# Attention and expert routing of layer 1 in one stage, routed batch by batch, with expert weights in the head buffers

## The chip, the cores and the metric

The kernel runs on one core of a Trainium2 chip. The metric is device time in microseconds (us) for one execution. Engine names are those of the profile: PE is TensorE (PEld its weight loads), DVE is VectorE, ACT is ScalarE, POOL is GpSimd, SP is SyncE, whose queue issues most DMAs.

## The reference

Four sub-layers follow one another on 4 x 1024 tokens of width 128: a Mamba mixer, a dense-routed expert layer, causal attention with 16 heads of 8, and a 64-expert top-4 layer. A layer norm follows each. The change touches the last two:

```python
scores = jnp.where(causal_mask, -1e9, einsum('bhqk,bhsk->bhqs', q, k) / sqrt(dk))
ctx = einsum('bhqs,bhsk->bhqk', softmax(scores), v)
x = layernorm(x + concat(ctx) @ Wo + bo)
top_p, top_i = top_k(softmax(x @ router_w), 4)
# slot of a (token, expert) pair: the count of earlier tokens that chose the expert
buf[expert, slot] = x[token]                     # 64 experts x 128 slots
y = (silu(buf @ w1[..., :64]) * (buf @ w1[..., 64:])) @ w2
x = layernorm(x + sum over the four chosen y * top_p)
```

## The kernel before, in words

The program is a chain of stages, each a block of its own with a barrier behind it. The last five are `attn_project` (941 to 1003 us), `attn_scores` (1003 to 1524), `out_and_route` (1524 to 1748), `moe_experts` (1748 to about 1845) and `moe_combine` (to 1903.7).

**`attn_scores`** handles 16 groups: group gi is 4 heads of batch gi // 4. The work of a group has two passes. The first pass finds row maxima: 39 items (`item`, L1762 and L1765 on PE into one of 3 PSUM banks; `first_pass`, L1688 on DVE reads the bank and frees it). It runs two groups ahead of the second pass. The second pass goes through 12 blocks of keys (`BLOCKS`, index n). For each block PE makes scores of two head pairs (`scores`, L1782), ACT takes their exponentials (L1665), POOL masks the 8 blocks on the diagonal (L1637), and PE multiplies with V three blocks later (`product`, L1797, `LAG` = 3). ACT copies the context of each half (L1654), PE turns it (`turn_context`, L1806), and DVE divides by the sums (`divide`, L1715 and L1719). PE's order is written out by `ring`: each block has four places x = 0 to 3, scores stand at 0 and 1, the product at 2, and the items are spread over all four; every other use of the 3 banks (the turned maxima, the turned contexts) has a fixed place too. PE works in program order, so any wait stops what is behind it. Batches 1 and 2 are two rounds of one hardware loop (`Fori` in `batches`); batches 0 and 3 are written out.

**`out_and_route`** then works on the four batches (quarters) one by one. PE turns the context (L2125), adds the bias with a one-row matmul (L2135) and multiplies by Wo (L2137). DVE adds the residual and norms (L2021 to L2035), PE turns again and makes the router's logits (L2148), and DVE finds the top four, the one-hot masks `oh`, the counts and the slots (`top_four`, `place`, `probabilities`, `share_beyond`), with two matmuls for running counts between (L2154, L2155). POOL scatters the quarter's rows to the DRAM tensor `slots`, one indirect DMA for each of 8 tiles x 4 choices (L1971): 32 a quarter, 128 in all. At the stage's start SP zeroes `slots` and loads w1 and w2, POOL clears w2's buffer (L1963), and small tables are made.

**`moe_experts`** loads `slots` (L2208) only behind the barrier, so it starts after the last scatter.

## Time and profile before

| | us |
|---|---|
| median of 3 runs (lowest, highest) | 1907.59 (1906.0, 1912.56) |
| the profiled execution | 1905.42 |
| its span | 1903.7 |
| attention stage | 1003 to 1524 |
| route stage | 1524 to 1748 |
| PE / DVE / ACT / POOL busy in the span | 1352.0 / 1315.3 / 881.0 / 842.4 |

The span is what the profiler sees between the first and the last instruction; the execution's own time is 1.7 us longer. The busy shares are means over very different stages, so the table of the row section that splits the span by stage says more. PEclk there is the granted TensorE clock: 1.00 is 2.4 GHz, 0.50 is 1.2 GHz.

### The profile page before, as it was taken

The numbers are of one execution on the slowest core, as the hardware profiler recorded it, in microseconds if no ns is written. First come the engines' busy times: TensorE is split into PE (matmuls) and PEld (weight loads), VectorE is DVE, ScalarE is ACT, GpSimd is POOL, SyncE is SP. The second block draws the span as 40 slices with busy tenths as digits, with TensorE's granted clock in tenths as the row PEclk, the third lists the DMA queues.
The fourth block names the chain that finished last, engine by engine and source line by source line (L and its number), as shares of the span: only waits on it lengthen the run. The fifth ranks groups of instructions, "written<-read, shape, count | busy, mean of one in ns | idle before, by whom it ended". The sixth has DMA issues, their size and how long they took to land. (4 is left out here: it accounts for less than half of the span.)

```text
span 1903.7 us, 27622 instructions
## 1 busy us (share of the span) xinstructions
PE 1352.0 (71%) x7253; PEld 734.7 (39%) x7253; DVE 1315.3 (69%) x2625; ACT 881.0 (46%) x1585; POOL 842.4 (44%) x930
## 2 busy tenths in 40 slices
PE   6847677677778669996236999999999944401637
PEld 2313333233333358996122344443444233201634
DVE  7999999999995351335648788887888167710315
ACT  5845565555655425563130566665666711101420
POOL 1666676666762045616430212121121217774750
PEclk8969999999999879998577899999999955555868
DMA  1000000000006226875052011010110091001315
GB/s 49 0 1 0 1 1 0 1 0 1 0 1 269 82 81 193 242 205 151 25 147 80 26 39 54 35 48 35 47 46 11 2 231 43 24 12 41 102 49 207
DMA packets 112117, 122.77 MB, mean 64 GB/s; under 512 B 28263, under 2 KB 87768, under 8 KB 108177
## 3 DMA queue, kind: packets, MB, share of 16 engines
q1 hardware_dynamic: 90480, 99.81, 17.0%
q0 software_dynamic: 10240, 15.79, 2.8%
q10 hardware_dynamic: 11264, 5.60, 1.0%
q8 instruction: 59, 0.97, 0.2%
q14 instruction: 74, 0.60, 0.1%
HBM read 76.62 MB, written 50.52 MB: 67 GB/s over the span
## 5 line engine op out<-in xcount | busy, mean ns | idle before, releaser
L1688 DVE TENSOR_REDUCE t_negm<-t_ps 128x1 f32<-128x512 f32 (+4 forms) x624 | 366.5, 640 | 63.3 <-PE t_ps L1765 39.9
L1665 ACT ACTIVATE t_PT<-t_ps_s 128x1024 f32<-128x1024 f32 (+3 forms) x384 | 293.1, 812 | 208.9 <-PE t_ps_s L1782 208.4
L435 POOL TENSOR_TENSOR s_HC<-s_H,s_C_sb 128x512 f32<-128x512 f32 x256 | 323.0, 1283 | 147.8 <-DVE s_H L523 125.7
L1637 POOL TENSOR_SCALAR_AFFINE_SELECT t_PT<-t_PT 128x512 f32<-128x512 f32 x128 | 80.5, 635 | 399.2 <-ACT t_PT L1665 399.2
L554 PE MATMUL ps_y<-s_HC,ident 128*128 128x512 f32 x512 | 252.0, 616 | 1.3 <-POOL s_HC L435 1.2
L1762 PE MATMUL t_ps<-c_K,c_Q 128*128 128x512 bf16 (+3 forms) x768 | 232.2, 341 | 27.5 <-DVE t_identb L1681 16.6
L473 ACT ACTIVATE s_dA<-m_DT,s_A 128x512 f32 (+1 forms) x256 | 169.9, 711 | 91.4 <-DVE s_H L523 91.1
L1782 PE MATMUL t_ps_s<-c_Q,c_K 128*128 128x512 bf16 (+3 forms) x768 | 181.9, 330 | 10.1 <-DMA c_Q<-max_parts 3.8
L540 PE MATMUL ps_b<-m_G,s_sel 128*128 (+1 forms) x128 | 74.3, 580 | 146.0 <-DVE s_H L523 125.4
L1971 POOL DMA_INDIRECT slots<-X,r_idx_s x128 | 129.4, 1011 | 82.4 <-issue 41.3
L1797 PE MATMUL t_ps_c<-t_PT,t_VG 128*32 128x512 f32 (+3 forms) x1536 | 163.4, 499 | 0.6 <-ACT t_CT L1654 0.6
L1762 PEld LDWEIGHTS t_ps<-c_K,c_Q 128*128 128x128 bf16 x768 | 74.3, 100 | 185.4 <-DVE t_negm L1688 133.9
L992 ACT ACTIVATE f_HT<-f_ps_h,f_b 128x128 f32<-128x128 f32 x340 | 96.5, 370 | 81.7 <-PE f_ps_h L1264 80.5
L554 PEld LDWEIGHTS ps_y<-s_HC,ident 128*128 128x128 f32 x512 | 101.4, 198 | 83.6 <-issue 64.2
L540 PEld LDWEIGHTS ps_b<-m_G,s_sel 128*128 128x128 f32 x128 | 25.6, 200 | 243.0 <-DVE s_H L523 183.1
L962 POOL DMA_INDIRECT f_YG<-expert_rows_out,f_idx_s x64 | 66.2, 1034 | 87.3 <-DMA expert_rows_out<-f_YB 68.7
L1765 PE MATMUL t_ps<-t_mask,t_identb 128*128 128x128 bf16 x512 | 104.4, 229 | 0.0
L1264 PE MATMUL f_ps_h<-f_XT,f_w 128*128 128x128 f32 x680 | 92.2, 280 | 8.1 <-issue 7.2
L1782 PEld LDWEIGHTS t_ps_s<-c_Q,c_K 128*128 128x128 bf16 x768 | 64.3, 98 | 72.8 <-ACT t_PT L1665 24.9
L1279 PE MATMUL f_ps_y<-f_w,f_HT 128*128 x680 | 89.8, 276 | 1.7 <-ACT f_HT L992 1.7
L1120 DVE COPY f_YB<-f_ps_y 128x512 f32<-128x512 f32 (+1 forms) x22 | 14.7, 669 | 109.1 <-PE f_ps_y L1279 100.6
L1264 PEld LDWEIGHTS f_ps_h<-f_XT,f_w 128*128 128x128 f32 x680 | 84.2, 195 | 9.8 <-issue 9.8
(323 smaller groups left out, 2525.2 us busy)
## 6 DMA issues: line engine op xcount, KB each, us to landing
f_w<-in_W_dram SPq DMA_DIRECT2D x93, 256.0 KB, 4.4
c_Q<-qk_parts SPq DMA_DIRECT2D x48, 192.0 KB
c_K<-qk_parts SPq DMA_DIRECT2D x48, 192.0 KB
token_expert_rows<-k_zero SPq DMA_DIRECT2D x8, 1024.0 KB, 10.2
y_Y<-token_expert_rows SPq DMA_DIRECT2D x8, 1024.0 KB, 7.9
qk_parts<-p_parts SPq DMA_DIRECT2D x48, 128.0 KB, 2.4
f_XS<-expert_rows SPq DMA_DIRECT2D x19, 256.0 KB
expert_rows_out<-f_YB ACTq DMA_DIRECT2D x19, 256.0 KB
```

Of the source, the lines that this page charges most:

```text
L435: nc.gpsimd.tensor_tensor(HC[:, g % RING, c, :], H[:, k, c, :], C_sb[:, k, :], ALU.mult).then_inc(s_hc, 1)
L473: nc.scalar.activation(dA[:, k, c, :], chunk2(DT, c, i), ACT.Exp, scale=A[:, c, g:g + 1]).then_inc(s_da, 1)
L540: nc.tensor.matmul(ps_b[k][:], sel[:, g, :], chunk(G, i), start=True, stop=True).then_inc(s_b, 1)
L554: nc.tensor.matmul(ps_y[c][:], ident[:], HC[:, g % RING, c, :], start=g == 0, stop=g == N - 1, skip_group_check=True).then_inc(s_y, 1)
L1264: mm = nc.tensor.matmul(ps_h[k % RH][:, m * P:(m + 1) * P], w1[:, k % RW, m * P:(m + 1) * P], XT[:, q % 2, a * P:(a + 1) * P], start=True, ...
L1665: nc.scalar.activation(PT[:, n % RP, 2 * p:2 * p + 2, 0:w], src, ACT.Exp, scale=DK ** -0.5).then_inc(s_exp, 1)
L1688: nc.vector.tensor_reduce(out, ps_1[bank][:, 0:h * width].rearrange("p (h k) -> p h k", h=h), AX.X, ALU.max, negate=True).then_inc(s_mx, 1)
L1762: mm = nc.tensor.matmul(ps_1[bank][:, u * width:(u + 1) * width], Q[g][:, j + u, qt * P:(qt + 1) * P], K[g][:, j + u, c * CH:c * CH + widt ...
L1765: mm = nc.tensor.matmul(ps_1[bank][:, (u + 1) * width - P:(u + 1) * width], identb[:], mask[:], start=False, stop=True, skip_group_check=True)
L1782: mm = nc.tensor.matmul(ps_s[p][:, h * CH:h * CH + w], K[g][:, 2 * p + h, kt * P:(kt + 1) * P], Q[g][:, 2 * p + h, c * CH + r * P:(c + 1) ...
L1797: mm = nc.tensor.matmul(ps_c[j * VW:(j + 1) * VW, r * P:CH], VG[:, g % 2, kt, j * VW:(j + 1) * VW], PT[:, n % RP, j, 0:w], start=kt == 0, ...
L1971: pool.indirect_dma_start(out=slots, out_offset=bass.IndirectOffsetOnAxis(ap=idx_s[:, j, t:t + 1].bitcast(U32), axis=0), in_=XM[:, t, :], ...
```

## The change

`attn_scores` and `out_and_route` become one stage, `attend_and_route`. The loop over batches 1 and 2 is gone: all 16 groups are written out. While batch q+1 is attended, batch q is routed, by this table: in group 0 of the next batch PE turns the context (before block 6) and multiplies by Wo (blocks 8 and 9), and DVE takes the statistics; in group 1 DVE norms, PE turns (before block 5) and makes the logits (block 7), and DVE chooses; in group 2 PE makes the counts (blocks 0 and 1) and DVE the slots. DVE does one step of a routine behind each use of a bank from the third on, and the rest of the routine at the group's end. The turned rows use the two score buffers `ps_s`; the other matmuls take turns in the 3-bank ring. POOL scatters one tile's choice per block, from group 2, block 6 on; what is left of the third batch follows the last group, then the clearing of w2, then the last batch's 32 scatters. The last batch is routed behind the last group with nothing beside it.

The bias is no longer a matmul: POOL adds `bo` to a batch's residual rows in group 1 of its own batch. ACT's table switches for the square root and back fall between exponentials. `slots` is zeroed in the attention stage behind the first maxima. The experts' w1 and w2 have no buffers of their own: w1 is loaded into the Q and K buffers of head groups 0 and 1 after the last batch's group 1, w2 into those of groups 2 and 3 after the last scores. The context rows and `oh` lie in the buffer `X2`. `moe_experts` and `moe_combine` are as before.

```diff
+ROUTE = [("out", 0, 0, 8, 3), ("out", 1, 0, 9, 3), ("logits", 0, 1, 7, 3), ("rank", 0, 2, 0, 3), ("rank", 1, 2, 1, 3)]
+TURN = [(0, 6), (1, 5)]
+TURNS = [(NG * (q + 1) + g, n) for q in range(BATCH - 1) for g, n in TURN]
+SCATTER = (2, 6)
...
+            if gi + 2 < TG:
+                uses += [("item", i, n, x) for i in range(NI * at // (4 * NB), NI * (at + 1) // (4 * NB))]
+            if at == 3 and gi + 1 < TG:
+                uses.append(("max", 0, n, x))
+            if x == 2 and n == LAG + 1 and gi:
                 uses.append(("context", 1, n, x))
             if x == 2 and n == LAG + 5:
                 uses.append(("context", 0, n, x))
+            if gi >= NG:
+                uses += [(kind, i, n, x) for kind, i, *when in ROUTE if when == [gi % NG, n, x]]
...
-        def batches(eng, body, first=0):
-            if first:
-                body(0, False)
-            with eng.Fori(first, BATCH - 1) as b:
-                body(b, False)
-            body(BATCH - 1, True)
...
+            maxima(0)
+            sp.wait_ge(s_m, 8)
+            for q in range(8):
+                rows = slots[q * (SLOTS // 8):(q + 1) * (SLOTS // 8), :].rearrange("(p a) n -> p (a n)", p=P)
+                sp.dma_start(rows, zero).then_inc(s_zb, 16)
+            for gi in range(TG):
+                b, g = gi // NG, gi % NG
+                if gi + 1 < TG:
+                    maxima(gi + 1)
+                sp.wait_ge(s_st, pair_use(gi, NB - 1) + 2)
+                if b + 1 < BATCH:
+                    sp.wait_ge(s_ml[g], b * 16 + 16)
+                    load_heads(sp, dram, keep, b + 1, g, dram["zeros"])
+                elif g == 1:
+                    for e in range(0, E1, GE):
+                        sp.dma_start(keep["w1"][:, e:e + GE, :], io["w1"][e:e + GE].rearrange("e d f -> d e f")).then_inc(keep["s_ew"], 16)
+            sp.wait_ge(s_zw, 1)
+            for q in range(2):
+                src = io["w2"].rearrange("(c q) i n -> q i c n", q=2)[q]
+                sp.dma_start(w2[q * I1:(q + 1) * I1, q:E1:2, :], src).then_inc(keep["s_ew"], 16)
...
+            def scatter(k):
+                q, t, j = k // (QTR * TOPK), k // TOPK, k % TOPK
+                if k == 0:
+                    pool.wait_ge(s_zb, 16 * 8)
+                if k % (QTR * TOPK) == 0:
+                    pool.wait_ge(s_x, q + 1)
+                    pool.wait_ge(s_nt, 2 * q + 2)
+                pool.indirect_dma_start(out=slots, out_offset=bass.IndirectOffsetOnAxis(ap=idx_s[:, j, t:t + 1].bitcast(U32), axis=0),
+                                        in_=XM[:, t, :], in_offset=None, bounds_check=SLOTS - 1, oob_is_err=False).then_inc(s_sc, 16)
+            sent = 0
+            for gi in range(TG):
+                for n, (c, kt, r) in enumerate(BLOCKS):
+                    if n == 2 and gi + 1 < TG:
+                        v_group(gi + 1)
+                    if n == 5 and gi % NG == 1:
+                        if gi < NG:
+                            pool.wait_ge(s_w, 48)
+                        rows = X[:, gi // NG * QTR:(gi // NG + 1) * QTR, :]
+                        nc.gpsimd.tensor_tensor(rows, rows, row_wide(bo[:], QTR), ALU.add).then_inc(s_bo, 1)
+                    if kt >= c * PER:
+                        pool.wait_ge(s_exp, pair_use(gi, n) + 2 + AHEAD)
                         part = PT[:, n % RP, :, 0:P]
                         nc.gpsimd.affine_select(out=part, in_=part, compare_op=ALU.is_ge, fill=0.0, base=0,
                                                 pattern=[[0, GH], [1, P]], channel_multiplier=-1).then_inc(s_mk, 1)
-            batches(pool, body)
+                    if gi * NB + n >= (NG * (sent // (QTR * TOPK) + 1) + SCATTER[0]) * NB + SCATTER[1]:
+                        scatter(sent)
+                        sent += 1
+            while sent < QTR * TOPK * (BATCH - 1):
+                scatter(sent)
+                sent += 1
+            pool.wait_ge(s_st, pair_use(TG - 1, NB - 1) + 2)
+            nc.gpsimd.memset(w2.rearrange("p e n -> p (e n)"), 0.0).then_inc(s_zw, 1)
+            while sent < QTR * TOPK * BATCH:
+                scatter(sent)
+                sent += 1
+            pool.wait_ge(s_sc, 16 * TOPK * NT)
...
+            def turned(q, k):
+                for p in range(2):
+                    act.wait_ge(s_st, turn_use(q, k) + p + 1)
+                    if k:
+                        act.wait_ge(s_p1, route_use(q, "out", p) + 1)
+                    elif q:
+                        act.wait_ge(s_p1, route_use(q - 1, "logits") + 1)
+                    nc.scalar.activation(CXT[:, p, :], ps_s[p][:, 0:CH], ACT.Copy).then_inc(s_exp, 1)
...
+                    if q >= 0 and (gi % NG, n) in TURN:
+                        turned(q, TURN.index((gi % NG, n)))
+                    if q >= 0 and (gi % NG, n) == (1, 0):
+                        root(q)
+                    if q >= 0 and (gi % NG, n) == (2, 0):
+                        route_exp(q)
...
+            for gi in range(TG):
+                q = gi // NG - 1
+                beside = normalise(q) if q >= 0 and gi % NG == 1 else iter(())
+                for k, (kind, i, *_) in enumerate(USES[gi]):
+                    use = BEGIN[gi] + k
+                    if kind == "item":
+                        first_pass(gi + 2, i, use)
+                    elif kind == "max":
+                        parts(gi + 1, use)
+                    elif kind == "context":
+                        divide(gi - i, i, use)
+                    elif kind == "out":
+                        projected(q, i, use)
+                        if i:
+                            beside = statistics(q)
+                    elif kind == "logits":
+                        logits_copy(q, use)
+                        beside = choose(q)
+                    elif i == 0:
+                        counts(q, use)
+                    else:
+                        positions(q, use)
+                        beside = place(q)
+                    if k >= 2:
+                        next(beside, None)
+                for _ in beside:
+                    pass
+            q = BATCH - 1
+            divide(TG - 1, 1, use_of(TG, "context", 1))
+            for h in range(2):
+                projected(q, h, route_use(q, "out", h))
+            for _ in statistics(q):
+                pass
+            for _ in normalise(q):
+                pass
+            logits_copy(q, route_use(q, "logits"))
+            for _ in choose(q):
+                pass
+            counts(q, route_use(q, "rank", 0))
+            positions(q, route_use(q, "rank", 1))
+            for _ in place(q):
+                pass
...
-def out_and_route(nc, io, keep, slots):
...
+            def turn_rows(q, k):
+                if k:
+                    pe.wait_ge(s_n, (q + 1) * QTR)
+                else:
+                    pe.wait_ge(s_mx, use_of(NG * (q + 1), "context", 1) + 1 + BANKS1)
+                for p in range(2):
+                    pe.wait_ge(s_exp, turn_use(q, k) + p - 1 + AHEAD)
+                    for t in range(PER):
+                        row = XM[:, q * QTR + p * PER + t, 0:P] if k else CX[:, q % 2 * QT + p * PER + t, :]
+                        mm = nc.tensor.transpose(ps_s[p][:, t * P:(t + 1) * P], row, ident[:])
+                    mm.then_inc(s_st, 1)
...
+            def project(q, h, use):
+                pe.wait_ge(s_w, 48)
+                pe.wait_ge(s_exp, turn_use(q, 0) + h + 1 + AHEAD)
+                pe.wait_ge(s_mx, use + 1)
+                for t in range(PER):
+                    mm = nc.tensor.matmul(ps_1[use % BANKS1][:, t * P:(t + 1) * P], CXT[:, h, t * P:(t + 1) * P], w[:], start=True, stop=True)
+                mm.then_inc(s_p1, 1)
...
+        QK = ctx.enter_context(nc.sbuf_tensor("heads", [P, 2 * NG, GH, SEQ], BF16))
+        flat = lambda lo, hi: QK[:, lo:hi].rearrange("p a j t -> p (a j t)").bitcast(F32)
+        half = 2 * QT * P
+        own = dict(keep, QK=QK, s_ew=ctx.enter_context(nc.semaphore("expert_weights")),
+                   w1=flat(0, NG).rearrange("p (e n) -> p e n", n=2 * I1), w2=flat(NG, 2 * NG).rearrange("p (e n) -> p e n", n=P),
+                   CX=keep["X2"][:, 0:half].rearrange("p (t n) -> p t n", n=P),
+                   oh=keep["X2"][:, half:T].rearrange("p (j t e) -> p j t e", j=TOPK, e=E1))
+        attention(nc, io, own, slots)
```

Three places show how instructions moved. The first is DVE in group 1 of a batch that has a batch to route (the third batch here), from the turned context of the first half on; `t_negm<-t_ps` is a first-pass item, `t_LG` the logits, `X` under L1916 the one-hot masks. Before, items follow one another:

```order
L1715 RECIPROCAL t_den<-t_ps 128x16
L1719 TENSOR_TENSOR CX<-t_ps,t_den 128x32 x4
L1688 TENSOR_REDUCE t_negm<-t_ps 128x4
L1688 TENSOR_REDUCE t_negm<-t_ps 128x2 x2
L1688 TENSOR_REDUCE t_negm<-t_ps 128x1 x8
L1693 TENSOR_TENSOR t_negm<-t_negm 128x4x4
```

Now:

```order
L1831 TENSOR_TENSOR X<-t_ps,t_den 128x32 x4
L1907 CAST t_idxf<-t_idx 128x64
L1908 TENSOR_TENSOR over<-t_LG,t_top 128x512
L1909 TENSOR_TENSOR t_ex<-t_top 128x32
L1911 COPY X<-t_idxf 128x8x4
L1798 TENSOR_REDUCE t_negm<-t_ps 128x4
L1916 TENSOR_TENSOR X<-t_iota,t_idxf 128x512 x2
L1798 TENSOR_REDUCE t_negm<-t_ps 128x2
L1916 TENSOR_TENSOR X<-t_iota,t_idxf 128x512 x2
L1798 TENSOR_REDUCE t_negm<-t_ps 128x2
L1921 TENSOR_TENSOR t_pair<-X 128x512 x2
```

One or two route steps now stand between each two items that PE waits to see read.

The second place is DVE in group 14, where no first-pass items are left. Before, the maxima of group 15 (L1700 to L1708) and then the divisions alone:

```order
L1702 CAST t_mp<-t_msb 32x128
L1704 TENSOR_TENSOR t_mrest<-t_msb,t_mp 32x128
L1706 CAST t_mp<-t_mrest 32x128
L1708 TENSOR_TENSOR t_mp<-t_mrest,t_mp 32x128
L1715 RECIPROCAL t_den<-t_ps 128x16
L1719 TENSOR_TENSOR CX<-t_ps,t_den 128x32 x4
```

Now, from the positions on:

```order
L1941 TENSOR_TENSOR t_pos<-t_ps,t_base 128x512
L1948 TENSOR_TENSOR X<-X,t_pos 128x512 x2
L1826 RECIPROCAL t_den<-t_ps 128x16
L1831 TENSOR_TENSOR X<-t_ps,t_den 128x32 x4
L1948 TENSOR_TENSOR X<-X,t_pos 128x512 x2
L1826 RECIPROCAL t_den<-t_ps 128x16
L1831 TENSOR_TENSOR X<-t_ps,t_den 128x32 x4
L1952 TENSOR_REDUCE t_posj<-X 128x32
```

The slots of the third batch (L1952 and what follows) come behind both divisions, the second of which waits for PE's block 8.

The third place is POOL at the end. Before, groups 14 and 15 had the masks and a copy alone, and the next stage began with its tables:

```order
L1637 AFFINE_SELECT t_PT<-t_PT 128x4x128 x8
L1620 COPY t_VG<-c_Vt 128x4x8 x8
L1637 AFFINE_SELECT t_PT<-t_PT 128x4x128 x14
L1528 UNCONDITIONAL_BRANCH
L1953 UNCONDITIONAL_BRANCH
L1955 MEMSET r_ones_row 1x128
```

Now, from the last diagonal blocks of group 15 on:

```order
L1713 AFFINE_SELECT t_PT<-t_PT 128x4x128
L1697 DMA slots<-X,t_idx_s 8192x140
L1713 AFFINE_SELECT t_PT<-t_PT 128x4x128
L1697 DMA slots<-X,t_idx_s 8192x140 x15
L1722 MEMSET heads 128x8192
L1697 DMA slots<-X,t_idx_s 8192x140 x32
```

A scatter stands behind each mask, and 14 scatters and the clearing of w2 stand ahead of the last batch's 32.

## Rows read from the trace of the kernel before

**Rows 1.** The table by stage; the columns are named in its first line.
```profile
core 0: us, PE busy (x) PEld busy (x) DVE busy (x) ACT busy (x) POOL busy (x), PEclk, DMA share, GB/s
...
1172.20:1290.90 118.70, 117.56 (x932) 49.62 (x932) 102.21 (x221) 76.53 (x105) 24.93 (x64) 1.00 0.12 44
...
1524.00:1574.00 50.00, 26.11 (x82) 17.48 (x82) 31.72 (x94) 8.39 (x12) 9.44 (x7) 0.54 0.87 220
1574.00:1676.00 102.00, 36.17 (x135) 26.33 (x134) 80.47 (x271) 15.26 (x24) 78.02 (x76) 0.52 0.10 32
```

**Rows 2.** Waits in four steady groups: total us, times, longest (DVE, weight loads).
```profile
DVE t_negm L1688 <- PE t_ps L1765: 8.0, 20, 0.6
...
PEld t_ps L1762 <- DVE t_negm L1688: 30.3, 49, 0.8
```

**Rows 3.** Timeline of SyncE: the first head load behind groups 7 and 8.
```profile
1290.97 0.77 SPq L1353 DMA_DIRECT2D c_Q<-qk_parts  x1
...
1325.83 0.80 SPq L1353 DMA_DIRECT2D c_Q<-qk_parts  x1
```

**Rows 4.** Timeline of the route stage's first quarter, setup and chain.
```profile
1527.14 6.92 POOL L1963 MEMSET experts_w<- 128x8192 f32 x1
1527.22 7.12 DVE L2000 CAST r_iota<-r_iota_i 128x512 f32<-128x512 int32 x1 [2.97 <-POOL r_trif L1961]
...
1534.86 1.94 PE L2125 MATMUL r_ps_t<-ident,CX 128*128 128x128 f32 x8 [11.42 <-DVE X L2004]
...
1536.73 2.07 PE L2135 MATMUL r_ps_o<-r_bo,r_ones_row 1*128 1x512 f32 x2
...
1537.45 1.28 ACT L1989 ACT_TABLE_LOAD   x1
...
1538.73 2.08 PE L2137 MATMUL r_ps_o<-r_w,r_CXT 128*128 128x128 f32 x8
...
1541.65 0.87 DVE L2024 BATCH_NORM_STATS2 r_stats<-X2t 128x6 f32<-128x128 f32 x4
...
1546.37 0.63 DVE L2027 BATCH_NORM_AGGREGATE r_mv<-r_stats 128x2 f32<-128x6 f32 x8
...
1547.71 2.13 DVE L2035 TENSOR_SCALAR X<-X2t,r_mv,r_rstd 128x128 f32<-128x128 f32 x8
...
1550.81 3.55 PE L2148 MATMUL r_ps_l<-r_router,r_CXT 128*128 128x64 f32 x16
...
1554.39 0.69 DVE L2041 COPY r_LG<-r_ps_l 128x512 f32<-128x512 f32 x1 [4.55 <-PE r_ps_l L2148]
...
1562.57 0.69 DVE L2086 TENSOR_TENSOR r_M<-r_pair 128x512 bf16<-128x512 f32 x1
...
1564.39 2.01 DVE L2090 TENSOR_TENSOR r_base<-r_base,r_ps_n 128x64 f32<-128x64 f32 x8 [1.13 <-PE r_ps_p L2155]
...
1575.12 1.30 POOL L1971 DMA_INDIRECT slots<-X,r_idx_s  x1 [41.06 <-DVE X L2061]
```

**Rows 5.** One tile, slots: the scatter, and the first load of the experts.
```profile
L1971 POOL DMA_INDIRECT slots<-X,r_idx_s x128: 981/982/1502, 1575.1 to 1744.8; - x128
L2208 SPq DMA_DIRECT2D e_x<-slots x16: 359/360/501, 1748.7 to 1804.7; - x16
```

**Rows 6.** Timelines of groups 14 and 15: POOL's masks, DVE, ACT.
```profile
1493.37 0.64 POOL L1637 TENSOR_SCALAR_AFFINE_SELECT t_PT<-t_PT 128x512 f32<-128x512 f32 x1 [10.49 <-ACT t_PT L1665]
...
1493.89 0.48 DVE L1719 TENSOR_TENSOR CX<-t_ps,t_den 128x32 f32<-128x32 f32 x4
...
1523.77 0.48 DVE L1719 TENSOR_TENSOR CX<-t_ps,t_den 128x32 f32<-128x32 f32 x4
...
1497.14 0.66 ACT L1665 ACTIVATE t_PT<-t_ps_s 128x256 f32<-128x256 f32 x2 [0.48 <-PE t_ps_s L1782]
...
1522.14 0.60 ACT L1673 ACTIVATE t_CT<-t_ps_c 128x512 f32<-128x512 f32 x1 [1.77 <-PE t_ps_c L1797]
```

**Rows 7.** One tile, r_zero: how long zeroing the slots takes to land.
```profile
DMA to landing us min/median/max: 2.8/5.2/6.9
```

770 lines of the change are left out of this document (330 added, 440 removed).

## Prediction

> **What bounds the kernel now.** I read the table by stage first, since the shares over the whole span mix unlike stages. The reader is to see two things in it. In attention TensorE is busy 117.56 of 118.70 us in four groups at a clock of 1.00, and VectorE 102.21 of them; a group takes 118.7 / 4 = 29.7 us, of which VectorE works 25.5 [rows 1]. In the route stage nothing is full: VectorE works 31.72 of 50 us and then 80.47 of 102, after which POOL alone is left with its scatters [rows 1]. The timeline of that stage shows its chain [rows 4]: tables, projection, norm, logits, choice, slots, and the first scatter at 1575.12. The rows of the tile slots give the rest: 128 scatters start from 1575.1 to 1744.8, so one in 169.7 / 127 = 1.34 us, and the experts' first load starts at 1748.7 [rows 5]. Attention ends with VectorE's last division at 1523.77 + 0.48 = 1524.3 [rows 6], so the route stage is 224.4 us of one engine waiting for another, half-clocked on TensorE (0.54 and 0.52) [rows 1].
>
> Attention must be read with the waits. TensorE is busy by the page, yet its weight loads waited 30.3 us in four groups for VectorE's reads of a bank, and VectorE 8.0 us (the largest of its waits) for the items [rows 2]. So the two are coupled through three banks: what is added to either shows in part.
>
> **What goes.** After the change only the last batch is routed outside attention. Its tail is a chain and 32 scatters.
> - The chain from the first turned context to the first scatter took 1575.12 - 1534.86 = 40.3 us [rows 4]. The tables ahead of it, 10.6 us of which 7.12 are one cast, are made in attention now, at its start, where VectorE is waited for by nothing late. The bias matmuls, 2.07 us for each half [rows 4], are gone, 4.1 in all; but VectorE now takes the first half's statistics (0.87) behind both additions and no longer beside the second half's product, so 3.2 off. TensorE comes out of attention at 1.00, so that the first turns (1.94) and one multiplication by Wo (2.08) [rows 4] may take half: 1.5 off, an estimate. Against that, clearing w2 now falls into the chain. Before, VectorE's cast started at 1527.22 beside POOL's clearing that started at 1527.14 and ran 6.92 us, and it took 7.12 [rows 4]: it ended 0.28 us after it. By POOL's order in the new program 14 scatters x 1.34 = 19 us come first, so the clearing meets the logits' copy and the top-four work. Bounds 0 and 6.9; I take 2, since most operations there are not of that cast's kind. Chain: 40.3 - 3.2 - 1.5 + 2 = 37.6.
> - Scatters: 31 x 1.34 = 41.4, and from the last one's start to the experts' load 1748.7 - 1744.8 = 3.9 [rows 5].
> - Tail 82.9 us against 224.4: **141.5 gained**.
> - Batches 1 and 2 were rounds of a hardware loop. The head loads behind groups 7 and 8 start 1325.83 - 1290.97 = 34.9 us apart [rows 3], where a group takes 29.7: the jump costs 5.2 us. Written out it goes: **5.2 gained**. The groups inside the loop take 29.7, as those of batch 0 do, so nothing else changes with it.
>
> **What is added to attention.** VectorE's route work for a batch is 31.72 + 80.47 us less 7.12 for the cast and 0.8 for small tables, over four: 26.1 busy [rows 1, 4]. With the gaps of its own chain it splits by the table of the change:
> - Group 0: two additions at 0.69, eight statistics (0.87 for four), 0.63 for their means and 0.17: 3.9 [rows 4].
> - Group 1: norm 2.4 (2.13 and a reciprocal), and from the logits' copy at 1554.39 to the end of M at 1563.26: 8.9. Together 11.3 [rows 4].
> - Group 2: from 1564.39 to the scatter at 1575.12, 10.7, and of the three last operations, 0.69 each, the part behind it, 1.3: 12.0 [rows 4].
>
> TensorE's part at half clock is 1.94 + 2 x 2.08 in group 0 and 2.14 + 3.55 in group 1 (2.14 is the second set of turns, taken as the first set plus 0.2) [rows 4]. At full clock that is 3.1 and 2.8, with a copy by ScalarE between each turn and the next scores, 0.6 (the context copy's time) [rows 6].
>
> A group has 29.7 us and VectorE needs 25.5 of it. With route work it needs 29.4, 36.8 and 37.5. Lower bound of a group's growth: 0 for the first, 7.1 and 7.8 for the others (VectorE never idle). Upper bound: all of it in a row, 3.9 + 3.7, 11.3 + 3.4 and 12.0 + 0.6. I stand near the lower: in the steps that are too long for the banks TensorE fills all three, which feed VectorE for 3 x 0.69 = 2.1 us, more than a product or a pair of scores takes between items. I take +4 (TensorE's own 3.7 lies there), +8.5 and +9: 21.5 for a batch, **43** for two.
>
> In the third, groups 0 and 1 cost the same 12.5. Group 2 is group 14, with no items to spread the work over. The slots of that batch come behind the second division, which ended at 1494.37 [rows 6]; then comes what is left of group 2's 10.7 us to the scatter once the counts (2.0), the positions (0.7) and four multiplications (4 x 0.69) are out [rows 4]: 5.3, to 1499.7. POOL stands at block 6 for it, and masks of blocks 8 to 11 are queued behind two scatters: the first mask would end at 1499.7 + 2 x 1.34 + 0.64 = 1503.0, where it ended at 1494.0 [rows 6]. PE's product wants it when block 11 is scored, about when ScalarE starts that block at 1497.1 [rows 6]: 5 to 6 us of stall, with the scores of group 15 behind it. From there a mask and a scatter take 2.0 us, as long as a wide block but more than a narrow one, which adds 2 to 3 by the last mask: **8** (bounds 4 and 13). Sum of the third: 20.5.
>
> ScalarE loads its tables twice more in a batch, 1.28 each [rows 4]; it works 76.53 of 118.70 us [rows 1], and in groups 1 and 2, where VectorE is the later one, that is covered. If VectorE were not late, it would cost up to 2.6 a batch. POOL's addition of the bias, on 128x1024 elements where a mask has half as many (0.64 [rows 6]), takes at least 1.3 us; four times that, 5 us, is my upper bound, and it stands among blocks 4 to 7, which need no mask: covered. In full batches a mask and a scatter (2.0 us) fit a block of 2.5: covered, by the three blocks that a product lags. Zeroing the slots lands within 6.9 us of its issue [rows 7] and the maxima of group 1 have some 20 us: covered; w1 and w2 land well before the tail's end. Three small loads ahead of the head loads: +1, an estimate.
>
> **Sum.** Attention +43 + 20.5 + 1 - 5.2 = +59.3; tail -141.5; together -82. The profiled execution took 1905.4, so 1823; the median of before stands 2.2 above it, so **1825**.
>
> **A row and a page against this change.** The row that speaks against overlapping VectorE with POOL is the cast of 7.12 us, which ended 0.28 us after a clearing of 6.92 us on POOL [rows 4]. It bears on the tail, where the sum has 2 us for it, and with the whole clearing it would have 6.9 and end at 1830. The Trainium skill, "SBUF — State Buffer", section "Who interferes with whom", says that the two engines share a pair of ports, held by one instruction for its whole length, by copies and casts of VectorE above all. By that page the operations of the top-four part that are copies or casts would wait for the clearing. The cast agrees with it; no row shows the other kinds beside POOL.
>
> **Rivals.**
> 1. *The gaps take it up.* VectorE idles 118.70 - 102.21 = 16.5 us in four groups [rows 1]. If all is used and TensorE's part is hidden, a batch grows by 26.1 - 16.5 = 9.6 to 11: attention 3 x 10 + 8 + 1 - 5 = +34, time 1800. Against it: groups 0 and 3 can't lend their gaps to 1 and 2. Chance 0.13.
> 2. *Nothing is covered.* Work of VectorE, TensorE and the table loads in a row: 27 + 7 + 2.6 = 37 a batch, 111 + 8 + 1 - 5 = +115, time 1881. For it: the coupling in [rows 2]. Against it: VectorE does not wait long anywhere. Chance 0.15.
> 3. *Masks and route steps collide.* A batch has fifteen 128x512 operations of VectorE that read two SBUF tiles, and if each waits for a mask (0.64 [rows 6]), that is 10 us a batch, 30 in all, time 1855. Masks fill 25 of 119 us on POOL [rows 1], so one in five would meet. Chance 0.07. The same section of the Trainium skill states this collision as a rule; no row here shows it.
> 4. *Scatters hold up TensorE: slower.* POOL's masks queue behind scatters. If a mask comes later than the three blocks that a product waits, each of the 96 scatters in attention moves TensorE by its whole 1.34 us: 129 on top of rival 2's 115: +244 - 141 = 2010. It decides from the point where a mask and a scatter together (2.0 us) exceed a block's time (2.5 us). Chance 0.03.
>
> **Chances.** The forecast has 0.62. Only rival 4 is slower. A measurement of this kernel tells 0.3% from no change. Faster 0.965, same 0.005, slower 0.03. The range takes in rival 1 and 3, 1798 to 1858, and leaves out rivals 2 and 4 with 0.18.
>
> **What would show it.** Right: groups of 33 to 34, 38, 38.5 and 29.7 us in batches 1 and 2, with VectorE over 95% busy in the second and third; no jump of 5 us between batches 1 and 2; POOL's first mask of group 14's last four some 8 us behind ScalarE; a tail of 83 us from the last division to the experts' load. Wrong: groups 1 and 2 of 30 to 35 us (rival 1), of over 43 (rival 2), or TensorE waiting for POOL in every batch (rivals 3 and 4).

## The result and the profile after

| | before | after |
|---|---|---|
| median of 4 runs, us | 1909.49 | 1853.22 |
| lowest, highest | 1906.0, 1912.56 | 1852.22, 1857.57 |
| span of the profiled execution | 1903.7 | 1851.0 |
| last division to the experts' first load | 224.4 | 85.9 |

The ratio is 0.9714, 95% interval 0.9700 to 0.9728: 56 us faster, where 82 were forecast. The time after lies inside the range, 28 us above the predicted 1825. The runs e1_unroll to e8_all below were timed while every kernel, before included, took some 130 us longer (before 2049 us), and e9_w2_late to e12_after_again while before took 1910, so runs are compared within these two sets, and by stage.

In the traces the last division of attention ends at 1609.64 where it ended at 1524.25: attention and what lies ahead of it are 85.4 us longer (59.3 forecast). The tail is 138.5 us shorter (141.5 forecast). The table by stage of the changed kernel comes first, cut where SP issues the next head loads, so one row is one group, 4 to 11, then groups 12 and 13, groups 14 and 15, and the tail. A group took 29.7 us before [rows 1]. The columns are the time and its length, then busy us (instructions) of PE, PEld, DVE, ACT and POOL, the granted clock, the DMA share and GB/s.

```profile
core 0: us, PE busy (x) PEld busy (x) DVE busy (x) ACT busy (x) POOL busy (x), PEclk, DMA share, GB/s
1176.54:1209.43 32.89, 32.38 (x257) 15.06 (x255) 27.74 (x65) 20.41 (x29) 6.26 (x16) 1.00 0.11 40
1209.43:1254.29 44.86, 37.54 (x258) 16.18 (x259) 38.77 (x113) 23.55 (x32) 8.84 (x17) 0.87 0.08 29
1254.29:1295.79 41.50, 34.42 (x236) 12.69 (x235) 36.07 (x81) 19.82 (x28) 12.69 (x21) 0.89 0.10 38
1295.79:1325.46 29.67, 29.34 (x234) 12.36 (x233) 25.43 (x57) 19.31 (x27) 18.07 (x29) 1.00 0.21 72
1325.46:1358.41 32.95, 32.39 (x257) 15.08 (x255) 27.80 (x65) 20.41 (x29) 17.98 (x29) 1.00 0.18 61
1358.41:1402.15 43.74, 36.80 (x258) 16.16 (x259) 38.70 (x114) 23.55 (x32) 13.49 (x21) 0.90 0.09 35
1402.15:1444.72 42.57, 34.69 (x236) 12.77 (x235) 36.19 (x81) 19.93 (x28) 12.66 (x21) 0.91 0.09 34
1444.72:1474.40 29.68, 29.34 (x234) 12.36 (x233) 25.45 (x57) 19.33 (x27) 18.07 (x29) 1.00 0.17 59
1474.40:1550.85 76.45, 68.56 (x515) 30.48 (x514) 66.07 (x176) 43.93 (x60) 30.30 (x49) 0.96 0.07 23
1550.85:1609.64 58.79, 47.96 (x349) 13.84 (x347) 19.69 (x61) 39.14 (x56) 31.82 (x44) 0.94 0.31 79
1609.64:1695.50 85.86, 9.80 (x50) 7.95 (x50) 29.48 (x91) 5.80 (x9) 51.09 (x46) 0.55 0.18 30
```

The growth sits in group 1 of a batch (44.9 and 43.7 us) and group 2 (41.5 and 42.6). VectorE has 38.7 us of work in the first and 36.1 in the second, so neither engine is full: VectorE stands idle for 5.0 to 6.4 us of each. TensorE, busy 29.3 us in a plain group, now shows 34 to 38 at a mean clock of 0.87 to 0.91; group 2 has almost the same matmuls, group 1 has 24 more for the routing. (With the clock at 1.00, in e10_even_last below, groups 5 and 6 show 32.6 and 31.0.) The waits of groups 5 and 6 together (us in all, times, the longest) show who waits:

```profile
PEld t_ps L2043 <- DVE t_negm L1798: 26.2, 28, 2.8
PE t_ps L2043 <- DVE t_negm L1798: 10.7, 10, 2.5
...
DVE t_negm L1798 <- PE t_ps L2046: 6.1, 8, 1.5
...
DVE t_negm L1798 <- PE t_ps L2043: 3.4, 6, 0.6
```

How one such wait goes is seen in group 5 at 1215. VectorE's order of time (start, us), then four slices of 4 us:

```profile
1215.48 1.11 DVE L1883 TENSOR_SCALAR X<-X2t,t_mv,t_rstd 128x128 f32<-128x128 f32 x4
1216.51 0.27 DVE L1809 COPY t_msb<-t_ps 32x128 f32<-32x128 f32 x1
...
1218.17 1.10 DVE L1883 TENSOR_SCALAR X<-X2t,t_mv,t_rstd 128x128 f32<-128x128 f32 x4
1219.20 2.06 DVE L1798 TENSOR_REDUCE t_negm<-t_ps 128x2 f32<-128x512 f32 x4
```

```profile
1214.00:1218.00 4.00, 3.20 (x31) 1.65 (x29) 3.51 (x12) 2.78 (x4) 1.27 (x2) 1.00 0.19 80
1218.00:1222.00 4.00, 2.07 (x15) 0.99 (x16) 3.82 (x10) 0.69 (x2) 0.00 (x0) 0.62 0.22 85
1222.00:1226.00 4.00, 4.00 (x19) 1.29 (x20) 2.08 (x3) 1.37 (x3) 3.78 (x11) 0.53 0.19 80
1226.00:1230.00 4.00, 4.00 (x30) 2.23 (x28) 3.20 (x9) 2.10 (x3) 1.03 (x1) 1.00 0.07 24
```

And TensorE in order of time, its wait, then a product of eight wide matmuls; the last line is such a product in a group of batch 0:

```profile
1219.93 0.50 PE L2043 MATMUL t_ps<-heads 128*128 128x384 bf16 x1 [2.48 <-DVE t_negm L1798]
...
1224.05 1.89 PE L2077 MATMUL t_ps_c<-t_PT,t_VG 128*32 128x512 f32 x8
...
1142.39 1.07 PE L2077 MATMUL t_ps_c<-t_PT,t_VG 128*32 128x512 f32 x8
```

Two norm steps with the maxima's chain between them fill 3.7 us, in which VectorE reads one bank only (the copy at 1216.51). TensorE fills its three banks and stands for 2.48 us. In slices of 1 us its granted clock is 0.97 at 1218, 0.50 from 1219 to 1225, and 1.00 again from 1226: it falls to 1.2 GHz while TensorE still stands, and stays there for some 6 us. In the last 4 of these TensorE is the later engine: the eight products take 1.89 us, not 1.07, and VectorE is busy for 2.08 us of 4. So this lump of route work costs twice, once as TensorE's wait and once as VectorE's wait for a half-clocked TensorE. The top four at 1245 to 1258 show the same. At the slots, 1265 to 1280, TensorE waits and the clock falls to 0.50 too, but VectorE is busy for 9.7 of the 10 us from 1270 on, so there the low clock costs nothing.

The low clock is not all of it. Of the 6.1 us that VectorE idles in group 5, 2.4 lie at half clock. Another 2.9 lie between 1228 and 1240 at a clock of 1.00: the norm is done, the logits are not there yet, TensorE is busy almost throughout, and VectorE's gaps hold no route work. So the work is too dense in one place and absent in another.

### The profile page after: what moved, and what is told of

Same layout as the page of the kernel before. It is cut to its first block and busy times, and to the rows that moved or that the text cites. A ratio compares the mean times of both kernels' runs of the same rounds, so it can differ in the third digit from the quotient of the medians.

```text
span 1851.0 us, 25866 instructions
## 1 busy us (share of the span) xinstructions
PE 1347.2 (73%) x7237; PEld 721.1 (39%) x7237; DVE 1312.3 (71%) x2628; ACT 883.2 (48%) x1585; POOL 853.5 (46%) x933
## 5 line engine op out<-in xcount | busy, mean ns | idle before, releaser
L1798 DVE TENSOR_REDUCE t_negm<-t_ps 128x1 f32<-128x512 f32 (+4 forms) x624 | 371.2, 641 | 68.0 <-PE t_ps L2046 38.6
L2043 PE MATMUL t_ps<-heads 128*128 128x512 bf16 (+3 forms) x768 | 239.3, 349 | 59.1 <-DVE t_negm L1798 39.0
L2062 PE MATMUL t_ps_s<-heads 128*128 128x512 bf16 (+3 forms) x768 | 185.7, 336 | 8.0 <-DMA heads<-max_parts 4.2
L2077 PE MATMUL t_ps_c<-t_PT,t_VG 128*32 128x512 f32 (+3 forms) x1536 | 172.2, 523 | 6.9 <-POOL t_PT L1713 6.3
L2043 PEld LDWEIGHTS t_ps<-heads 128*128 128x128 bf16 x768 | 74.7, 101 | 229.7 <-DVE t_negm L1798 164.2
L1697 POOL DMA_INDIRECT slots<-X,t_idx_s x128 | 126.9, 992 | 76.1 <-DVE X L1964 43.4
L992 ACT ACTIVATE f_HT<-f_ps_h,f_b 128x128 f32<-128x128 f32 x340 | 96.7, 371 | 82.9 <-PE f_ps_h L1264 81.6
L2062 PEld LDWEIGHTS t_ps_s<-heads 128*128 128x128 bf16 x768 | 66.0, 101 | 73.7 <-ACT t_PT L1774 22.3
L1120 DVE COPY f_YB<-f_ps_y 128x512 f32<-128x512 f32 (+1 forms) x22 | 14.7, 670 | 111.2 <-PE f_ps_y L1279 97.2
```

The lines of the kernel that those rows point to most:

```text
L1697: pool.indirect_dma_start(out=slots, out_offset=bass.IndirectOffsetOnAxis(ap=idx_s[:, j, t:t + 1].bitcast(U32), axis=0), in_=XM[:, t, :], ...
L1798: nc.vector.tensor_reduce(out, ps_1[use % BANKS1][:, 0:h * width].rearrange("p (h k) -> p h k", h=h), AX.X, ALU.max, negate=True).then_inc ...
L2043: mm = nc.tensor.matmul(out[:, u * width:(u + 1) * width], Q[g][:, j + u, qt * P:(qt + 1) * P], K[g][:, j + u, c * CH:c * CH + width], sta ...
L2062: mm = nc.tensor.matmul(ps_s[p][:, h * CH:h * CH + wd], K[g][:, 2 * p + h, kt * P:(kt + 1) * P], Q[g][:, 2 * p + h, c * CH + r * P:(c + 1) ...
L2077: mm = nc.tensor.matmul(ps_c[j * VW:(j + 1) * VW, r * P:CH], VG[:, g % 2, kt, j * VW:(j + 1) * VW], PT[:, n % RP, j, 0:wd], start=kt == 0, ...
```

## The experiments

In the first set most of the 130 us lies ahead of attention: the first head load is issued at 1194 us in e2_group14 and at 1088 in the changed kernel. The first groups of attention, which have no route work, kept their 29.6 us. But groups 7 and 11 took 30.7 and group 8 36.8 in e2_group14, where the changed kernel has 29.7 and 33.0; e9_w2_late of the second set, with the same edit, has 29.7 and 33.0 again. So that excess isn't from an edit, and its cause stays open.

**The loop written out, alone** (kernel before).

```diff
-            if first:
-                body(0, False)
-            with eng.Fori(first, BATCH - 1) as b:
-                body(b, False)
-            body(BATCH - 1, True)
+            for b in range(BATCH):
+                body(b, b == BATCH - 1)
```

> The kernel before with its attention loop over batches 1 and 2 written out, nothing else. By the prediction's term the back edge goes: 5.2 us less (ratio 0.9973), head loads behind groups 7 and 8 29.7 us apart and no longer 34.9, all other groups 29.6 to 29.7. Rival: the longer program loses as much in loading its code; then 0 in all, and single groups or the stage's start are longer.

Ratio 0.9988 (0.9963 to 1.0013), too coarse for 5 us. The trace tells it: SP's head loads behind groups 7 and 8 start at 1405.73 and 1435.35, 29.6 us apart, where they were 34.9 [rows 3], and all other groups take 29.6. So the jump of 5.2 us is gone from the trace, and no group is longer. Whether the stage's start pays something for it can't be told, since before has no trace in this set.

**Slots of batch 2 at once.**

```diff
                         positions(q, use)
                         beside = place(q)
+                        if gi + 2 == TG:
+                            for _ in beside:
+                                pass
```

> The changed kernel, with the slots of batch 2 made at once behind the positions in group 14 (that group has no items between which the steps could lie), not step by step behind later uses. If TensorE's 5.7 us wait for a mask in group 14 is from the slots being late, the first scatter of that batch starts 5 to 8 us earlier, the wait falls under 2 us, and the kernel is 5 to 8 us faster than the changed kernel's 1853 (1845 to 1848). Rival: the mask and scatter pace of 2.0 us sets the length of groups 14 and 15 in any case; then the wait moves on to later blocks and the kernel stays within 2 us of 1853.

Groups 14 and 15 take 52.0 us and no longer 58.8. POOL's scatter, which stood 16.32 us for the slots in the changed kernel, stands 7.08. First the changed kernel, then this one (start, us, and in brackets the idle time before it):

```profile
1576.87 1.38 POOL L1697 DMA_INDIRECT slots<-X,t_idx_s  x1 [16.32 <-DVE X L1964]
...
1579.52 0.65 POOL L1713 TENSOR_SCALAR_AFFINE_SELECT t_PT<-t_PT 128x512 f32<-128x512 f32 x1
...
1580.23 1.93 PE L2077 MATMUL t_ps_c<-t_PT,t_VG 128*32 128x512 f32 x8 [5.73 <-POOL t_PT L1713]
```

```profile
1680.82 1.38 POOL L1697 DMA_INDIRECT slots<-X,t_idx_s  x1 [7.08 <-DVE X L1964]
...
1663.59:1715.60 52.01, 46.63 (x349) 13.58 (x347) 19.50 (x60) 39.08 (x56) 31.67 (x44) 0.99 0.33 89
```

The scatter pace was not the bound there. TensorE's longest wait for a mask in these groups is 0.65 us, where it was 5.73. The rival falls, and 6.8 us are won. This kernel is the base of what follows.

**Steps further apart.** The base here is the changed kernel; a step runs behind every second use in group 1 and every fourth in group 2.

```diff
+EVERY = {1: 2, 2: 4}
...
-                    if k >= 2:
+                    if k >= 2 and k % EVERY.get(gi % NG, 1) == 0:
                         next(beside, None)
```

> The changed kernel, with a route step behind every second use of a bank in group 1 and every fourth in group 2, not behind every one: the same work, spread over the group. Lumps: route steps that come one after another starve TensorE, which then runs at half clock, so spreading them takes groups 6 and 10 from 41.5 and 42.6 us to 37 or 38 (VectorE's busy time there is 36), and 8 to 11 us off the kernel (1842 to 1845). Rival, additive: VectorE and TensorE pass three banks to and fro, so each us of route work shows wherever it stands; then groups 5, 6, 9, 10 keep their lengths within 1 us and the kernel stays at 1853. In both cases group 14, which has few uses, gets its slots later, 3 to 8 us worse.

Groups 5 and 6 of e2_group14, then of this kernel:

```profile
1315.72:1359.43 43.71, 36.47 (x258) 15.88 (x259) 38.73 (x113) 23.54 (x32) 8.82 (x17) 0.90 0.08 29
1359.43:1402.15 42.72, 34.71 (x236) 12.69 (x235) 36.13 (x81) 19.92 (x28) 12.67 (x21) 0.90 0.10 37
```

```profile
1317.54:1354.47 36.93, 33.04 (x257) 14.87 (x257) 33.17 (x105) 23.29 (x32) 8.55 (x17) 1.00 0.09 35
1354.47:1396.72 42.25, 33.36 (x236) 13.00 (x237) 40.94 (x89) 20.34 (x28) 10.84 (x21) 0.96 0.10 38
```

The first theory forecast 37 or 38 us for groups 6 and 10; they took 42.3 both, so it had the place wrong. The additive rival had groups 5 and 9 unchanged, and it fails too. The pair went from 86.4 to 79.2 us with the same work: the end of the top-four part (the last compares, the sums and M) slipped from group 5 into VectorE's time of group 6 (33.2 and 40.9 us busy in place of 38.7 and 36.1), VectorE's idle time fell from 11.6 us to 5.1, and the clock in group 5 is 1.00. Groups 9 and 10 took 39.6 and 42.3. This is group 9:

```profile
1463.01:1502.63 39.62, 35.72 (x257) 15.52 (x257) 33.47 (x105) 23.42 (x32) 12.14 (x21) 0.91 0.11 38
```

It has nearly the busy time of group 5 on VectorE (33.5 and 33.2 us), and in both TensorE stands for 1.4 us at the norm, before 1327.0 and before 1472.5. But in group 5 the clock stays at 1.00, and in group 9 it is 0.50 from 1474 to 1479, and the group is 2.7 us longer. That is the price of one fall of the clock by itself, as far as one pair of groups can show it. At it the two falls that begin in group 5 of the changed kernel come to some 5 us, an estimate. What e3_spread won in these groups it lost in groups 14 and 15, 65.6 us, as expected; the median is the same as that of e2_group14 (1977.3 and 1976.9).

**More VectorE work.**

```diff
                     also(nc.vector.tensor_tensor(oh[:, j], iota[:], wide(idxf[:, :, j], E1), ALU.is_equal))
+                    link(nc.vector.tensor_tensor(M[:], iota[:], wide(idxf[:, :, j], E1), ALU.is_equal))
...
+                    link(nc.vector.tensor_tensor(pair[:, 1], iota[:], pos[:], ALU.mult))
                     also(nc.vector.tensor_tensor(oh[:, j], oh[:, j], pos[:], ALU.mult))
```

> The changed kernel, with four more compares of 0.68 us (into a buffer that is overwritten) in the choice of a batch (group 1) and four more products of 0.69 us in its slots (group 2): 2.7 us more in each. Additive: groups 5, 9 and 13 grow by 2.7 each, groups 6, 10 and 14 by 2.7, the tail by 5.5: +22 us, 1875. Clock: each added us of VectorE also keeps TensorE waiting and lowers its granted clock, so groups grow by 4 or more each and the kernel by 30 or more. Gaps: VectorE was idle for 5 to 6 us of such a group, so under half of it shows in attention: +14 or less.

```profile
1321.64:1368.67 47.03, 36.79 (x258) 16.00 (x259) 41.75 (x117) 23.54 (x32) 8.81 (x17) 0.87 0.07 27
1368.67:1415.41 46.74, 37.02 (x236) 13.52 (x235) 39.99 (x85) 19.92 (x28) 13.15 (x21) 0.80 0.09 34
```

VectorE's busy time rose by 3.0 and 3.9 us (each added operation also waits for its own end), the groups by 3.3 and 4.0, and the tail by 5.7. In batch 3, groups 12 and 13 took 83.7 us (76.9 in e2_group14) and 14 and 15 60.5 (58.8 in the changed kernel): 8.5 for the same 6.9. The median, 2010.2, stands 33.3 above e2_group14, and 6.8 of that are its faster group 14: so 26.5 us for 4 x 6.9 = 27.6 us of work. Additive: at the margin a us of VectorE costs a us, nothing is covered, and nothing is amplified over the whole. That holds for work put where VectorE is already dense; it doesn't say what the same work costs elsewhere.

**w2 cleared ahead of the scatters.**

```diff
-            while sent < QTR * TOPK * (BATCH - 1):
-                scatter(sent)
-                sent += 1
             pool.wait_ge(s_st, pair_use(TG - 1, NB - 1) + 2)
             nc.gpsimd.memset(w2.rearrange("p e n -> p (e n)"), 0.0).then_inc(s_zw, 1)
```

> The edit of e2_group14, and POOL clears w2's buffer ahead of the 14 scatters that are left of batch 2, not behind them. Ports by kind of operation: the clearing (7 us) then lies beside VectorE's last divisions, additions and statistics, none of them a copy or a cast between two SBUF buffers; nothing waits, the cast of 4.0 us in the top-four part of the tail goes back to 0.2, and from the last division to the experts' first load it takes 82 us and no longer 86. Rival: any operation of VectorE that reads SBUF is held up by the clearing; then the 4 us come back as one long addition or statistics and the tail stays at 86.

It got worse, 88.7 us from the last division to the load. In the changed kernel the clearing and the cast meet as in the kernel before [rows 4]; the cast lasts until the clearing ends:

```profile
1626.00 6.96 POOL L1722 MEMSET heads<- 128x8192 f32 x1
```

```profile
1625.40 0.69 DVE L1891 COPY t_LG<-t_ps 128x512 f32<-128x512 f32 x1 [6.42 <-PE t_ps L2115]
1626.13 1.11 DVE L1898 MAX8 t_top<-t_LG 128x8 f32<-128x64 f32 x8
...
1628.97 4.04 DVE L1907 CAST t_idxf<-t_idx 128x64 f32<-128x64 uint32 x1
```

In this run the clearing (1710.95 to 1717.9) lengthens nothing beside it, a division and two additions, and the cast lasts 0.19 us, as the first theory has it; but VectorE stands idle in front of it, with the clearing long over (that wait is 4.25 of the 6.3 us by which this tail exceeds that of e9_w2_late):

```profile
1738.01 0.19 DVE L1904 CAST t_idxf<-t_idx 128x64 f32<-128x64 uint32 x1 [4.25 <-DMA a_dt_b<-in_dt_b_dram]
```

**And w2's load held back.**

```diff
             sp.wait_ge(s_zw, 1)
+            sp.wait_ge(s_x, BATCH)
             for q in range(2):
```

> e5_clear_first with the load of w2 held back until the last batch's slots are made (in e5_clear_first it ran 12 us beside the last norm and logits, and VectorE then stood still for 4.25 us in front of the top-four part's cast, when the clearing was long over). If the load is the cause (it fills the DMA engines, and what VectorE waits for, its own program's code among it, comes late), VectorE starts that cast at once, and from the last division to the experts' first load it takes 82 us and no longer 89. If the cause is the row of scatters on POOL, which end 0.6 to 2.4 us ahead of the cast's start in e5_clear_first and e8_all, the 3 to 4 us stay and it takes 86 or more.

```profile
1621.91 0.20 DVE L1905 CAST t_idxf<-t_idx 128x64 f32<-128x64 uint32 x1
...
1602.64:1685.13 82.49, 9.39 (x49) 7.95 (x50) 26.18 (x91) 5.80 (x9) 50.93 (x47) 0.55 0.19 32
```

No idle time before the cast, and 82.5 us of tail. But that the load is the cause isn't shown, because the two runs with the wait (e5_clear_first, and e8_all with 2.98 us) are of the first set and the two without it (this one and e11_best) of the second. Two things in the traces speak against it. In the changed kernel the same 2 MB moved from 1633 to 1645 beside VectorE's compares and products, and VectorE never stood for more than 0.67 us there. And in e2_group14, e3_spread, e4_double and e7_even, all of the first set, VectorE stood for 1.3 to 2.6 us in front of the second addition of the tail with its input made, where no such load ran (DMA share 0.04 to 0.06); the second set has 0.04 us there. In e7_even the last product ends at 1710.58:

```profile
1708.02 2.56 PE L2133 MATMUL t_ps<-t_w,t_CXT 128*128 128x128 f32 x16
...
1712.13 0.69 DVE L1877 TENSOR_TENSOR X2t<-X2t,t_ps 128x512 f32<-128x512 f32 x1 [1.72 <-remote]
```

So VectorE can stand like that without the load. e5_clear_first run again in the second set would decide it. What VectorE missed stays open: the tensor that the row of e5_clear_first names has nothing to do with it, and e8_all has "remote" there.

**Three operations on POOL.** The last three of `place` for batches 0 to 2 (`ex * total`, `beyond`, `ex * beyond`) become four on POOL, behind the masks' place in blocks 4 to 7 of group 3.

> The edit of e2_group14, and for batches 0 to 2 the last three operations of the slots' part (0.69 us each: probabilities divided, beyond capacity, product) leave VectorE; POOL does them in four operations among blocks 4 to 7 of group 3, where it has no masks. Additive: groups 6 and 10 go from 42.7 to 40.5 us and group 14 is not changed: 4 us less in all. Amplified: they lie at a place where TensorE starves and loses its clock, so 3 us or more a group come back, 6 to 8 in all. Rival: POOL's operations hold VectorE's up through SBUF, groups 7, 11 grow by as much as 6, 10 shrink.

Groups 6 and 10 took 39.8 and 40.0 us (42.7 and 42.6 in e2_group14), groups 7 and 11 29.7 and 29.7 (30.7 both), the median is 4.2 us less. So 3.6 to 4 us a batch for 1.9 us of VectorE's time; but group 9 took 45.0 us (43.7) and groups 12 and 13 79.9 (76.9), and groups 6 and 10 with nothing edited in them came out at 41.3 to 42.7 in other runs, so the excess over "additive" is not settled. POOL's 5.5 us in group 7 hold nobody up. In group 15, where masks and scatters leave POOL no room, they do: groups 14 and 15 take 54.5 us and no longer 52.0, which no theory had.

**Steps laid evenly.** Routines carry over a group's end; one operation a step; steps by this table:

```diff
+RANKS = [(2, 4), (2, 5), (2, 0), (2, 1)]
+SCATTERS = [(3, 4), (3, 4), (2, 6), (0, 0)]
...
+def pace(gi, kind):
+    if gi // NG == BATCH - 1:
+        return 1
+    return {"choose": 2, "place": 3}.get(kind, 1)
...
-                    if k >= 2:
+                    if k >= 2 and use % pace(gi, what) == 0:
                         next(beside, None)
```

> The edit of e2_group14, and the route steps of batches 0 and 1 laid evenly: one operation of about 0.7 us a step, a choice step behind every second use of a bank from group 1 on into group 2, the two count matmuls at blocks 4 and 5 of group 2 and not 0 and 1, a slot step behind every third use, into group 3, scatters from group 3, block 4. The work is the same. Lumps theory: VectorE's busy time, 26 + 4 x 25.5 = 128 us a batch, is the only bound; the four groups of a batch, 152 us together in e2_group14, take 135 to 142, with TensorE's clock at 1.00 throughout, and the kernel is 20 to 30 us faster than e2_group14. Additive rival: each us of route work shows wherever it stands; then the four groups stay at 150 to 152 together, the lengths only move from groups 5 and 6 to 7.

Batch 1 (groups 4 to 7) took 32.9 + 38.8 + 36.5 + 33.2 = 141.4 us, where e2_group14 has 150.0; batch 2 36.9 + 37.6 + 37.8 + 34.5 = 146.8 for 153.9. The additive rival falls: same work, 15.7 us less in the two, though the median is only 12.6 less (1964.3) and not 20 to 30. The clock isn't 1.00 throughout (0.91 in group 5): a wait of 2.5 us at the norm is left, whose steps still had four operations.

> e7_even with the edits of e5_clear_first and e6_pool_share together. If the three are independent, it is e7_even less 4 us of tail and less 2 us a batch for the three operations that leave VectorE: 8 us faster than e7_even. If TensorE's order and no longer VectorE is the bound there, the three operations bring nothing and it is 4 us faster.

1959.0, 5.3 us less than e7_even, where 8 were expected if all was independent. Groups 7 and 11 lose 1.4 and 3.2; the tail stays (86.9), since e5_clear_first's new wait is in it, and POOL's operations cost 3 in groups 14 and 15.

**Batch 2 evenly too.** `RANKS` for it at blocks 2 and 3, its scatters from block 7, `pace` for it as for the others, and two operations a step in the norm.

> e7_even with batch 2 laid evenly too: its choice behind every second use in group 13, what is left of it in group 14 (which has no items), its count matmuls at blocks 2 and 3 of group 14, its first scatter at block 7; and the norm in steps of two operations in all batches. Lumps: group 13 goes from 44.2 us to 38 or 39, groups 14 and 15 keep their 54 within 2, and groups 5 and 9 lose the 2.5 us wait at the norm: 38.8 and 37.6 go to 36 or 37. In all 6 to 9 us off e7_even (1964). Rival: the later counts move the slots of batch 2 and with them the masks of group 14's second half, and the 5 us come back as a wait of TensorE for POOL there.

1826.0 where before takes 1910.7, and 15.1 us less than e9_w2_late beside it, although that one has the better tail by 4.8. Groups 5 and 9 took 35.6 and 35.5 us at a clock of 1.00, groups 12 and 13 68.9 together for 76.9, groups 14 and 15 55.7 for 52.4. So 8 us are won in group 13, 3 of them come back as the rival has it. The norm's standstill, 2.5 and 2.4 us in groups 5 and 9 of e7_even with a fall of the clock behind each, is down to 1.4 and 1.3 with none, and the groups are 3.2 and 2.1 us shorter (across the two sets).

**All that held.** e10_even_last with the clearing first, the load held back, and the three operations on POOL for batches 0 and 1 alone; beside it the changed kernel once more.

> e10_even_last with the three tail and POOL edits: the clearing ahead of the scatters left of batch 2, the load of w2 behind the last batch's slots, and the last three operations of batches 0 and 1 on POOL in group 3. Tail: from the last division to the experts' load 83 us as in e9_w2_late and no longer 87.7. Groups 7 and 11 lose 2.07 us of VectorE each and take 31 and 33, not 33.2 and 35.1. Together 8 to 9 us off e10_even_last, if the parts are independent. Rival: with VectorE spread, TensorE's own work (31 of 33 us) bounds groups 7 and 11, POOL's operations bring nothing, and only the tail's 4.7 us are gained.

> The changed kernel once more, beside e11_best, so that the two stand on the same chip: group lengths as in its first profile (32.9, 44.9, 41.5, 29.7, 33.0, 43.7, 42.6, 29.7) within 1.5 us each, and e11_best 33 to 36 us faster.

1818.05 us against 1853.26 of the changed kernel and 1909.78 of before (ratio to before 0.9516, 0.9503 to 0.9529): 35.2 us better than the change. Its groups 4 to 7 and its tail:

```profile
1173.94:1206.84 32.90, 31.86 (x253) 15.06 (x255) 27.74 (x65) 20.40 (x29) 6.23 (x16) 1.00 0.11 40
1206.84:1242.43 35.59, 32.56 (x254) 14.96 (x259) 31.66 (x97) 23.20 (x32) 8.77 (x17) 1.00 0.10 36
1242.43:1278.88 36.45, 30.98 (x233) 12.36 (x237) 35.94 (x85) 19.98 (x29) 8.10 (x16) 1.00 0.10 36
1278.88:1310.68 31.80, 29.71 (x231) 12.30 (x233) 28.38 (x66) 19.32 (x26) 18.42 (x27) 1.00 0.15 54
...
1571.83:1654.37 82.54, 9.39 (x49) 7.95 (x50) 26.29 (x91) 5.80 (x9) 51.87 (x48) 0.55 0.19 32
```

Group 6 is now at what the forecast had called the lower bound, VectorE never idle: it is busy 35.9 of 36.5 us. Groups 7 and 11 (31.8 and 31.3) fell as expected, so the rival that TensorE bounds them is out. The second run of the changed kernel has the group lengths of the first within 0.3 us, but for 43.6, 42.6 and 41.4 in groups 5, 6 and 10, and 59.8 in groups 14 and 15 (44.9, 41.5, 42.6 and 58.8). So a single such group is known to about 1.3 us.

## Why the prediction was right in sign and 28 us off

- **Tail, forecast 82.9, measured 85.9.** Right in mechanism. The chain to the first scatter took 39.4 us, not 37.6, because clearing w2 cost 3.9 us and not the 2 taken between the bounds 0 and 6.9 (cast of 4.04 us for 0.18). Scatters start 1.37 us apart on average, not 1.34, 1 us over 31. In e9_w2_late, where the clearing lies ahead of the top four, the tail is 82.5.
- **Back edge, 5.2 gained.** Right, by the trace of e1_unroll.
- **Group 0 of a batch, +4.** Measured +3.2 and +3.3.
- **Group 1, +8.5.** Measured +15.2 and +14.1: this is the term that failed. The prediction had the upper bound 11.3 + 3.4 = 14.7 and stood near the lower, since the three banks that TensorE fills during a long step would feed VectorE for 2.1 us after it. It took VectorE's side alone and put TensorE's standing at nothing. The trace shows that side: during 3.7 us of steps TensorE stands for 2.5, comes back at 1.2 GHz, and VectorE then waits for it; and between the norm and the logits VectorE's gaps go unused. Even steps took it away (groups 5 and 9 at 35.6 and 35.5 us in e10_even_last). By the pair of groups in e3_spread a fall of the clock costs 2.7 us by itself, so it is a part of the miss and not all of it; the rest is the uneven placing, which no run separates further.
- **Group 2, +9.** Measured +11.8 and +12.9, upper bound 12.6. The waits are of the same kind, though of the two stretches at 1.2 GHz in group 6 only the first makes VectorE wait.
- **Batch 3, +20.5.** Groups 12 and 13 grew by 17.2 (12.5 forecast, again the group 1 term), groups 14 and 15 by 8.5 (8 forecast). POOL's scatter stood for the slots and TensorE 5.73 us for the first mask behind it, as told; e2_group14 took the wait away.
- **Start, +1.** Measured +4.3 at the first head load, of which 3.1 lie ahead of the attention stage, in code the change doesn't touch. In the five traces of changed kernels where before takes 1910 that load starts anywhere from 1085.1 to 1089.3, so the 1 us can't be told.

The misses add up to 29 us: group 1 three times (6.7, 5.6, 4.7), group 2 twice (2.8, 3.9), the start 3.3, the tail 3.0, groups 14 and 15 0.5, less 1.5 in group 0. That is the miss in the span, 1851.0 against 1903.7 - 82.2 = 1821.5; between the medians it is 28, since the forecast carried 2.2 us from the profiled execution to the median of before.

That the time fell into the range is in part luck. It lies as far from rival 2 (1881) as from the forecast, and the upper end, 1858, was drawn to take in rival 3, which didn't happen. By the prediction's own signs of being wrong, group 1 (44.9 and 43.7, "over 43") fell on rival 2's side, and VectorE was 86 to 87% busy in groups 5 and 6, not over 95%. The tail and the back edge, which make the change faster at all, were right by mechanism.

The rivals: rival 1 would have made a batch 129 us long; with even steps e11_best comes to 136.7 (groups 4 to 7), the changed kernel to 149. Rival 2 (nothing covered) was the nearest for groups 1 and 2, and had 0.15; in all it has 37 us a batch where 30 were measured, because group 0 grew by 3.2 us and not by 7.6, and because the table loads (2.6) were covered. Rival 3 falls in size, but its collision is real. The compares and products of batches 0 to 2 (shortest, median and longest, ns) show little:

```profile
L1916 DVE TENSOR_TENSOR X<-t_iota,t_idxf x12: 674/677/679, 1246.5 to 1545.8; 128x512 f32<-128x512 f32 x12
L1948 DVE TENSOR_TENSOR X<-X,t_pos x12: 674/691/1114, 1266.0 to 1563.4; 128x512 f32<-128x512 f32 x12
```

But by their times none of the 12 compares ran beside a mask, and only two of the products did (0.75 and 1.11 us in place of 0.69). Where another such operation met a mask, the mask could be the one to last longer, as here beside the two sums, and it made nobody wait:

```profile
1398.01 1.28 DVE L1921 TENSOR_TENSOR t_pair<-X 128x512 f32<-128x512 f32 x2
...
1398.04 1.74 POOL L1713 TENSOR_SCALAR_AFFINE_SELECT t_PT<-t_PT 128x512 f32<-128x512 f32 x1 [4.29 <-ACT t_PT L1774]
```

Before, no mask took over 0.67 us; now six of 128 take 0.77 to 1.74. The Trainium skill, "SBUF — State Buffer", section "Who interferes with whom", has such operations contend with a GpSimd instruction that reads SBUF; the trace agrees wherever the two met. It cost little because they seldom met: some 5 us over the three batches on both engines together, an estimate from the durations above the usual ones, about half of it on masks, which have three blocks of lag. The section also says that a VectorE operation in a two-port mode, which casts can enter, is blocked for the whole length of a GpSimd instruction that came first, and that operations with one SBUF input outside these modes pass. The 4.04 us cast beside the 6.96 us clearing agrees with the first, and MAX8, 1.11 us beside that clearing, with the second. Rival 4 falls in full batches (groups 3 of a batch, with a mask and a scatter in most blocks, take 29.7 us).
